# Where the output bias of four attention blocks is added: on VectorE after the projection, or on GpSimd ahead of it

## The reference, cut to what matters

```python
def _mha(q_in, kv_in, ...):
    q, k, v = heads(q_in, wq, bq), heads(kv_in, wk, bk), heads(kv_in, wv, bv)
    attn = softmax(einsum('bhqd,bhkd->bhqk', q, k) / sqrt(16))
    return einsum('bhqk,bhkd->bhqd', attn, v).reshape(B, S, D) @ out_w.T + out_b

x = x + _mha(_ln(x), _ln(x) or the context, ...)
```

## Time and profile before

| | |
|---|---|
| time, median of 3 runs | 1947.57 us (1942.87 to 1950.38) |
| the profiled execution's own time | 1943.69 us |
| its span in the trace | 1941.9 us, so 1.8 us lie around it |
| busy share of the span | PE 90%, DVE 67%, ACT 43%, POOL 36% |
| the last chain of waits, by engine | PE 55%, DVE 23%, issue 10%, POOL 5%, ACT 4% |
| mean granted clock of PE | 0.965 |
| one batch of the loop, update to update, mean | L0_sa 11.5, L0_ca 26.6, L1_sa 12.8, L1_ca 20.3 us |

### The profile page before, as it was taken

The page is one execution under the profiler, slowest core; times in us unless marked ns, Lnnn a source line. Parts: engine busy times, 40 slices in busy tenths (PEclk is TensorE's granted clock), DMA queues, the critical chain, the costliest instruction groups (busy, mean ns, idle before and its releaser), DMA issues.

```text
span 1941.9 us, 35088 instructions
## 1 busy us (share of the span) xinstructions
PE 1740.7 (90%) x11106; PEld 1239.9 (64%) x11106; DVE 1297.7 (67%) x3310; ACT 842.2 (43%) x2473; POOL 704.9 (36%) x796
## 2 busy tenths in 40 slices
PE   5979998889997879999799999998988989998998
PEld 4756665679986668666685455585545855565577
DVE  5866777511127886888765665897778967566665
ACT  3645555333334642656324444343233445444431
POOL 2325555230012234667332333340001445454543
PEclk9989999789998989999999999999999999999999
DMA  4100000288972000012100020101001000000200
GB/s 175 33 24 17 17 8 16 78 287 323 326 253 98 1 0 22 31 46 75 69 11 17 17 73 0 55 1 66 1 0 69 9 1 23 14 12 12 77 1 19
DMA packets 37015, 115.22 MB, mean 59 GB/s; under 512 B 3344, under 2 KB 23728, under 8 KB 29728
## 3 DMA queue, kind: packets, MB, share of 16 engines
q1 hardware_dynamic: 34352, 107.33, 15.8%
q0 software_dynamic: 2544, 6.43, 1.0%
HBM read 99.34 MB, written 14.40 MB: 59 GB/s over the span
## 4 chain that ended last, share of the span: by engine, by line
PE 55%; DVE 23%; issue 10%; POOL 5%; ACT 4%; DMA 1%; DVEq 1%; POOLq 0%; SPq 0%; ACTq 0%
PE ps L1060 7%; PE ps L1100 5%; PE ps L862 5%; PE ps L938 4%; PE ps L1210 4%; PE ps L1222 4%; PE ps L993 4%; POOL arena L2111 4%; PE ps L971 3%; PE ps L910 3%; PE ps L857 3%; PE ps L966 2%; DVE arena L1787 2%; PE ps L835 2%; PE ps L915 2%
## 5 line engine op out<-in xcount | busy, mean ns | idle before, releaser
L2111 POOL TENSOR_TENSOR arena<-arena,rinv 112x375 f32<-112x375 f32 (+1 forms) x448 | 370.8, 830 | 461.7 <-DVE rinv L1770 449.5
L938 PEld LDWEIGHTS ps<-cst,arena 112*125 112x125 f32 (+1 forms) x1408 | 186.5, 181 | 168.1 <-POOL arena L2111 83.7
L938 PE MATMUL ps<-cst,arena 112*125 112x112 f32 (+1 forms) x1408 | 245.0, 291 | 39.3 <-POOL arena L2111 35.8
L1343 ACT ACTIVATE arena<-ps,negmax 112x375 f32<-112x375 f32 (+1 forms) x384 | 190.6, 501 | 153.5 <-DVE negmax L1765 153.1
L1779 DVE COPY arena<-ps 125x336 f32<-125x336 f32 x384 | 190.4, 496 | 44.3 <-PE ps L938 43.4
L1765 DVE TENSOR_REDUCE negmax<-ps 112x1 f32<-112x375 f32 (+1 forms) x288 | 158.1, 549 | 64.7 <-PE ps L910 57.4
L1343 ACT ACTIVATE arena<-arena,negmax 112x112 f32<-112x112 f32 (+1 forms) x256 | 125.6, 491 | 143.3 <-DVE negmax L1754 96.5
L1060 PE MATMUL ps<-h_split_sb,w_split_sb 128*128 128x448 f32 x768 | 171.7, 370 | 6.9 <-POOL w_split_sb L2187 3.0
L1060 PEld LDWEIGHTS ps<-h_split_sb,w_split_sb 128*128 128x128 f32 x768 | 144.7, 190 | 23.5 <-POOL w_split_sb L2187 4.9
L857 PE MATMUL ps<-wat,arena 128*125 128x256 f32 (+1 forms) x576 | 142.7, 385 | 2.4 <-DVE arena L1673 1.5
L2187 POOL TENSOR_TENSOR w_split_sb<-wml,w_split_sb 128x512 fp32r<-128x512 f32 (+1 forms) x40 | 46.9, 1171 | 233.9 <-ACT w_split_sb L1409 232.0
(11 more groups left out here) (230 smaller groups left out, 3264.3 us busy)
## 6 DMA issues: line engine op xcount, KB each, us to landing
wml<-in_wm_L_moe SPq DMA_DIRECT2D x21, 1028.0 KB, 6.9
wml<-in_wm_L_moe SPq DMA_DIRECT2D x21, 1024.0 KB, 7.9
craw<-in_ctx SPq DMA_DIRECT2D x32, 375.0 KB
wml<-in_wm_L_m SPq DMA_DIRECT2D x3, 3072.0 KB, 14.3
wat<-in_wa_L_ca SPq DMA_DIRECT2D x2, 2560.0 KB, 9.3
wml<-in_wm_L_m SPq DMA_DIRECT2D x2, 2048.0 KB, 10.2
keys_hbm<-arena SPq DMA_DIRECT2D x8, 375.0 KB
arena<-keys_hbm SPq DMA_DIRECT2D x8, 375.0 KB
```

The costliest lines, as they stand in the source:

```text
L938: last = nc.tensor.transpose(ps[0:blk.kp, T_BANK + s % blk.t_banks, o:o + S], buf[:, i * blk.nk + q * blk.kp:i * blk.nk + (q + 1) * blk.kp ...
L1343: last = go(probs[0:S, s % blk.nprobs, i * nk:(i + 1) * nk], src[:, i * nk:(i + 1) * nk], ACT.Exp, scale=-1.0 if blk.mask == "input" else ...
L2111: pool.tensor_tensor(p3, p3, r3, ALU.mult).then_inc(scaled, 1)
```

## The change

In the four blocks with an output bias, GpSimd adds the bias to X[:, m] in place, once DVE has signalled that batch m is normalised (`xn_ready`). For m = 0 it does so ahead of the block's first `scale`, for m = b+1 in step 1 of body b, ahead of `scale(b, 1)`. A new semaphore `biased` counts these additions. `update` is one DVE operation for all blocks, X <- PSUM, X; where there is a bias it waits for `biased` too. The counts of DVE's own links are adapted, since `update` has none now.

```diff
@@ starts()
+            at["bi"] += B * (blk.out_bias is not None)
@@ semaphores
+        biased = sem("biased")
@@ DVE, update(b)
                     dve.wait_ge(out_full, count(st["out"], 1, b, 1))
                     W = ps[0:S, blk.out_bank, blk.out_at:blk.out_at + D]
                     if blk.out_bias is not None:
-                        links[0](v.tensor_tensor(xo[:, 0], W, bias_rows[0:S, blk.out_bias], ALU.add))
-                        v.tensor_tensor(xs(b), xo[:, 0], xs(b), ALU.add).then_inc(out_done, 1)
-                    else:
-                        v.tensor_tensor(xs(b), W, xs(b), ALU.add).then_inc(out_done, 1)
+                        dve.wait_ge(biased, count(st["bi"], 1, b, 1))
+                    v.tensor_tensor(xs(b), W, xs(b), ALU.add).then_inc(out_done, 1)
@@ DVE, links of the bodies
-                cu = int(blk.out_bias is not None)
+                cu = 0
...
+                    elif c0 == 0:
+                        link = Links(start + rest[0])
@@ GpSimd, attention(n)
+                def add_bias(m):
+
+                    pool.wait_ge(xn_ready, count(st["xn"], 1, m, 1))
+                    one = X[:, m] if isinstance(m, int) else X[:, bass.ds(m.i * 2 + m.o, 1)].rearrange("p o d -> p (o d)")
+                    pool.tensor_tensor(one, one, bias_rows[0:S, blk.out_bias], ALU.add).then_inc(biased, 1)
+
                 order = [x for s in sorted(blk.pool) for x in blk.pool[s]]
                 for name in order:
                     prepare(name, 0)
+                if blk.out_bias is not None:
+                    add_bias(0)
 
                 def body(b):
                     for s in steps(b, blk, 0):
                         if more(b):
                             for name in blk.pool.get(s, []):
                                 prepare(name, b + 1)
+                            if blk.out_bias is not None and s == 1:
+                                add_bias(b + 1)
                         scale(b, s)
```

More of the change, by code:

```diff
@@ L194, in starts @@
 def starts():
-    at = dict(ws=0, hs=0, spread=0, w=0, w0=0, w1=0, w2=0, w3=0, turn=0, pair=0, out=0, xn=0, cn=0, unit=0, masked=0, group=0, o=0, qk=0, kn=0, ctx=0, mask=0, ff=0, silu=0, clip=0, xt=0, hh=0, wat=0, wml=0)
+    at = dict(ws=0, hs=0, spread=0, w=0, w0=0, w1=0, w2=0, w3=0, turn=0, pair=0, out=0, xn=0, cn=0, unit=0, masked=0, group=0, o=0, qk=0, kn=0, bi=0, ctx=0, mask=0, ff=0, silu=0, clip=0, xt=0, hh=0, wat=0, wml=0)
     rows = []
```

## The result

The changed kernel takes 1923.31 us (1920.56 to 1926.93) and the one before 1948.97 us (1942.87 to 1952.12) on the same chip: a ratio of 0.9872, 95% interval 0.9846 to 0.9897.

A forecast was written before the change was run, and what follows sets the result against it. Neither DVE nor POOL was taken to bound the kernel everywhere, so each block was read separately. Updates saving 12.9 us less 4.55 us for delayed cnorms gave 8.3 us, from 1947.57 to 1939.2 us; range 1932 to 1944, with spread 1945.

The forecast's parts named there:

- The sum: Whole kernel: 12.9 us saved by the updates less 4.55 us lost in L0_ca, 8.3 us faster.
- the written-out bodies: Bodies 7 and 8 of the four changed blocks, outside the loops: 3.15 us saved together, ends 2.7 and 3.4.
- Where DVE waits for PE, 0.35: Loop updates in L0_sa, L1_ca and L0_ca: each saves 0.35 us behind PE's projection, ends 0.25 and 0.43.
- L1_sa, 0.57: L1_sa's loop: DVE is last, so each of six updates saves the full 0.57 us, 3.4 us together.
- The next wait behind DVE stays the same one: Behind each update: statistics move along with it, and the same next wait remains, only shorter.
- less than the 0.4: L1_sa's loop: a period falling by less than 0.4 us would show the prediction wrong.
- The addition, 0.71 us: POOL: each of 32 additions takes 0.71 us, hidden in L0_sa, L1_sa and L1_ca.
- L0_ca, 0.65 us per batch for the cnorms: L0_ca: the addition and following scale on POOL delay DVE's cnorms by 0.65 us, seven times, 4.55 us.
- another of the prediction's signs of being wrong: L0_ca's loop: the batch was to rise by 0.3 us from 26.6; a shorter one would show the prediction wrong.
- Rival A: L0_ca: the cnorms lose nothing, cost near 0, gain 12.9 us, 1934.7 us; chance 0.22.
- Rival B: L1_ca and L0_ca: updates are not what ends last, their loops give nothing, gain 4.1 us, 1943.5; chance 0.11.
- Rival C: L1_ca and L0_ca: GpSimd becomes the bound of both, 14.7 us slower, 1962; chance 0.05.

The follow-up runs named there:

- e1: The changed kernel with 9 tiny memsets on DVE ahead of its first wait; 1935.55 us, ratio 0.9934 to the kernel before.
- e2: The kernel before the change with 119 tiny memsets on DVE ahead of its first wait; 1939.29 us, ratio 0.9953.
- e8: The changed kernel itself, run once more beside the version with the cross blocks' addition in step 6; 1923.94 us, ratio 0.9866.
- e9: The changed kernel with L1_sa's statistics behind each update taken over 128 of the 256 columns; 1922.86 us, ratio 0.9857.
- e4: The changed kernel with no addition on POOL, the update waiting for `xn_ready` instead, output bias left out; 1922.23 us, ratio 0.9871.
- e3: The changed kernel with the cross blocks' addition in step 6 instead of step 1; 1921.99 us, ratio 0.9869.
- e5: The changed kernel with 64 tiny memsets on DVE ahead of its first wait; 1941.24 us, ratio 0.9961.
- e6: The changed kernel with 4 tiny memsets on DVE ahead of its first wait; 1935.01 us, ratio 0.9921.

## Why the prediction was wrong

**The step that failed is "The sum".** It adds what the four blocks gain and takes 1943.69 - 8.3, so it holds the other blocks as they were because their code is unchanged. L3_ca gave 10.2 us of the 20.2 by its place alone. e1 takes 12.2 us away again by 9 memsets and e2 gives before 9.2 us by 119. The trace of the kernel before had the row: an idle of over 3 us with "issue" behind both returns of a loop, in a kernel from which the change takes static instructions ahead of that loop. No term and no rival had it.

**The edit by itself.** With the stall in both, before and e1 are 1948.97 and 1935.55, 13.4 us (12.9 against the 1948.49 of before beside e1); without it, e2 and the changed kernel are 1939.29 and 1923.31, 16.0. The profiled executions show 10.2 us up to L2_ca. The runs of one kernel are spread over up to 11 us, and the traces show some of that: from the first update of L0_sa to that of L2_ca the changed kernel and e8, the same code, take 1007.5 and 1004.9 us, before and e2 take 1017.3 and 1014.8; from there to L3_ca, where nothing was changed, the changed kernel takes 562.5 and e8 565.4. The profiled executions of before and e2 are also 5.3 and 4.3 us under their medians, the changed kernel's is at its own, and between e2's and the changed kernel's there are 11.5 us and not 16.0. What makes the longer executions of before and e2 longer no trace shows. At equal placement 8.3 was two to eight microseconds too small. That e1's 1935.55 lies in the range is in part luck: the prediction's terms miss in both directions, as follows.

By its terms, in the profiled executions: the loops' six updates each give 6 x (0.46 + 0.20 + 0.35 + 0.37) = 8.3 us, and the rest of the 10.2, 1.9, lies outside the loops. I had 3.15 for the written-out bodies; 1.9 can't be told from the 2.6 by which equal code differs over that stretch, so this term stays unchecked.

- *Where DVE waits for PE, 0.35.* The mechanism held, the lag behind the projection was mis-sized: 0.15 us in L0_sa and L0_ca (forecast 0.25), so 0.46 is saved, beyond the end of 0.43. I charged 0.08 for the second wait, and it costs nothing that shows. In L1_ca the lag is 0.24 and 0.37 is saved, and PE's hole is 0.74 (forecast 0.75).
- *L1_sa, 0.57.* Wrong, and it was the one place where I did not ask what comes next behind the gain. DVE's own chain is 0.57 shorter, and PE's scores take over after 0.35 (e9). "The next wait behind DVE stays the same one" is false here, and the period falls by less than the 0.4 that the prediction itself named as a sign of being wrong.
- *The addition, 0.71 us.* 0.73 measured. Free in L0_sa, L1_sa and L1_ca (e4), each as argued.
- *L0_ca, 0.65 us per batch for the cnorms.* Shown in kind, mis-sized: 0.26 (e3, e4). The addition starts 0.3 us earlier behind DVE's rinv than I put it, since its address is ready, and the scale follows it without the 0.15 that I charged for the issue. So the first cnorm meets only the addition's rest (470 ns), and the second pays for the scale as forecast, with 896 ns and not over 1 us. L0_ca became 0.20 shorter where I had it 0.3 longer, another of the prediction's signs of being wrong.
- *Rival A* is half right: gain and loss both exist, and the gain wins. *Rival B*: both ca loops gave their share. *Rival C*: POOL bounds nothing new.
- *The Trainium skill's advice* (GPSIMD Engine Reference, "Engine selection") against elementwise additions on GpSimd: 0.73 us on POOL against 0.42 for DVE's addition of the bias, slower as it says, and worth it here since POOL's time is free.

## What to carry to other kernels

Read the idle times with "issue" at the head of hardware loops before an edit: the loop of 321 instructions here paid 3 to 7 us per return for its place, and any edit ahead of such a loop that changes the number of instructions, however small, moves that place. So a gain or loss of some tenths of a per cent is not the edit's until a copy with the same placement (a few instructions that do nothing, on the same engine, ahead of everything) has been timed; the per-batch periods of each loop tell in one table whose it is. And where the slowest engine of a step is relieved, the gain ends at the next arrival, which has to be read beside it.

## What was unexpected in the hardware

- Place alone is worth 9 to 18 us of 1923 (e2, e1, e5): 3.3 us per return with 14 instructions left in the last unit of 128, 3.6 with 19, 7.4 where the loop touches four units (there in two parts, at the branch and behind the first register steps), none with 23 left. The batches lose more than the stall (3.66 and 6.02 us before, 9.2 and 8.5 in e5). I did not settle why: PE waits only 2.92 us for what DVE releases behind the second stall of before. I did not settle either why the second long batch costs more than the first in before, and less in e1, e5 and e6.
- POOL works out the address of the next operation while the current one runs; the addition follows with no gap (62.97 behind 62.08 + 0.93). DVE's step before X takes 0.15 to 0.24 us behind PE's end with two waits on register counts, where it takes 0.17 with one.
- Of DVE's cnorms queued against POOL, one slips in between two POOL operations (470 ns for 402 alone), the next is held for the whole of the following one (896).
